# Four graph-network layers on one core: attention weights transposed by DMA bands and VectorE blocks instead of by TensorE

## What is computed

```
L0: e = lrelu((h W1)(h W2)^T), masked by adj; softmax over rows;   relu(attention @ (h W3))
L1: 4 heads, e = lrelu(e_src + e_dst), masked; softmax;            elu(attention @ (h W))
L2: 4 heads, e = Q K^T / 8, masked; softmax;                       layernorm((attention @ V) Wo + bo) * gamma + beta
L3: as L1, with weights and vectors of its own
```

## Time and profile before

| | |
|---|---|
| median of 3 runs | 2933.38 us (2931.53 to 2934.24) |
| the profiled execution, its own time | 2927.78 us |
| its span, first to last instruction | 2926.0 us |
| mean granted TensorE clock | 0.996 |
| DMA packets, bytes | 58840, 109.89 MB |

### The profile page before, as it was taken

One profiled execution on the slowest core, in us unless ns is written; L12 is line 12 of the kernel. 1 busy time (PEld: TensorE's weight loads), 2 busy tenths in 40 slices (PEclk: granted clock), 3 DMA queues, 4 the chain that ended last, 5 costly groups with the idle time before them and its releaser, 6 DMA issues.

```text
span 2926.0 us, 68155 instructions
## 1 busy us (share of the span) xinstructions
PE 2872.5 (98%) x27764; PEld 2045.5 (70%) x27764; DVE 2134.2 (73%) x5596; ACT 1667.6 (57%) x3554; POOL 790.4 (27%) x917
## 2 busy tenths in 40 slices
PE   6899999999999999999999999999999999999988
PEld 5567777767767767767767767767767667767666
DVE  3677877777877777877777877777777777777764
ACT  2456656556656656656656656656656655655633
POOL 2223222323222333222322222323222323222321
PEclk9999999999999999999999999999999999999999
DMA  3011011011011101011101011101011101011000
GB/s 81 24 36 43 24 45 45 33 35 45 24 45 44 37 31 45 23 45 45 38 30 44 23 45 45 38 30 45 23 45 45 37 31 44 23 45 38 30 23 30
DMA packets 58840, 109.89 MB, mean 38 GB/s; under 512 B 5568, under 2 KB 41408, under 8 KB 58528
## 3 DMA queue, kind: packets, MB, share of 16 engines
q1 hardware_dynamic: 58032, 104.61, 10.9%
q0 software_dynamic: 496, 0.92, 0.3%
HBM read 88.21 MB, written 17.30 MB: 36 GB/s over the span
## 4 chain that ended last, share of the span: by engine, by line
PE 94%; DVE 2%; DMA 1%; ACT 1%; issue 1%; POOL 0%; SPq 0%; POOLq 0%; DVEq 0%; ACTq 0%
PE ps L962 20%; PE ps L1069 17%; PE ps L968 11%; PE ps L1095 8%; PE ps L998 8%; PE ps L1128 8%; PE ps L1104 8%; PE ps L1018 8%; PE ps L948 4%; PE ps L1007 2%; PE ps L1115 1%; PE ps L956 1%; DMA hT<-r_dram 1%; DVE pA L746 0%; DVE stats L634 0%
## 5 line engine op out<-in xcount | busy, mean ns | idle before, releaser
L452 ACT COPY hT<-ps 128x1024 f32<-128x1024 f32 x128 | 129.6, 1012 | 431.9 <-PE ps L948 431.9
L746 DVE SCALAR_TENSOR_TENSOR pA<-qT,gval,adjT 128x512 f32<-128x512 f32 x248 | 202.6, 856 | 208.8 <-DMA hT<-r_dram 208.1
L384 POOL TENSOR_TENSOR qx<-qx,xc 128x512 f32<-128x512 f32 x128 | 174.6, 1364 | 647.5 <-ACT qx L524 647.5
L1069 PEld LDWEIGHTS ps<-vals,pA 128*64 128x64 f32 x8192 | 253.9, 139 | 53.1 <-issue 52.8
L1069 PEld LDWEIGHTS ps<-vals,pB 128*64 128x64 f32 x8192 | 249.3, 138 | 59.0 <-issue 59.0
L443 ACT ACTIVATE hn<-xc,nb,rstd 128x256 f32<-128x256 f32 x384 | 202.5, 595 | 140.4 <-DVE nb L651 140.4
L359 POOL TENSOR_SCALAR rstd<-mv 128x4 f32<-128x4 f32 x160 | 37.2, 232 | 880.7 <-DVE mv L643 880.7
L1069 PE MATMUL ps<-vals,pA 128*64 128x65 f32 x8192 | 265.4, 223 | 5.9 <-DVE pA L746 5.9
L1069 PE MATMUL ps<-vals,pB 128*64 128x65 f32 x8192 | 267.0, 224 | 1.0 <-DVE pB L746 1.0
L962 PE MATMUL ps<-wgat,hT 128*128 128x264 f32 x1024 | 255.0, 393 | 0.4 <-ACT hT L452 0.4
L1095 PE MATMUL ps<-qx,qT 64*128 64x512 f32 x1024 | 250.5, 615 | 1.5 <-ACT qx L548 0.9
(11 more groups left out here) (147 smaller groups left out, 6097.3 us busy)
## 6 DMA issues: line engine op xcount, KB each, us to landing
qT<-r_dram SPq DMA_DIRECT2D x64, 512.0 KB, 4.0
hT<-r_dram SPq DMA_DIRECT2D x64, 512.0 KB, 4.9
x_in<-in_x SPq DMA_DIRECT2D x32, 512.0 KB, 3.9
out_x<-xc SPq DMA_DIRECT2D x32, 512.0 KB, 3.0
pX<-in_adj SPq DMA_DIRECT2D x1, 1024.0 KB, 7.2
r_dram<-growT SPq DMA_DIRECT2D x64, 8.0 KB, 1.4
pX<-in_L_gnn_W SPq DMA_DIRECT2D x2, 256.0 KB, 4.7
pA<-in_L_gnn_a POOLq DMA_DIRECT2D x8, 64.0 KB, 7.4
```

Of the source, the lines that this page charges most:

```text
L746: last = nc.vector.scalar_tensor_tensor(out=gat_p[s][h % 2][:, t, :], in0=row, scalar=gval[s][:, 1, t, h:h + 1], in1=adjT[:, t, :], op0=AL ...
L1069: last = nc.tensor.matmul(ps[lo:hi, BANK[f"G{g}.{h}"], t * DV:(t + 1) * DV], gat_p[s][h % 2][:, j, t * P + lo:t * P + hi], vals[s][:, j, h ...
```

## The change

The weights of layer 0 and of heads 2 and 3 of layer 2 are no longer transposed by TensorE. SyncE moves each finished matrix to a scratch tile in 16 DMAs, one for each pair of bands: 32 partitions by one 32-column block out of each 128, which puts every 32 x 32 block where its transpose belongs. VectorE then transposes inside the 32 x 32 blocks, four instructions of 128 x 512 per matrix, back into the tile that held the weights. The scratch of layer 0 and of head 2 is `pB` of the set; head 3 has a new tile `scratch`. Heads 0 and 1 stay with TensorE. `growT` becomes one tile per GAT layer instead of one per set. All banks and the order of all five engines' lists are new; part of layer 3's `gat_norm` and `gat_aggregate` move from c to d, a slot later. In the lists below `...` marks what is left out; the old lists stand above.

```diff
-        probT2 = [[pX[2], pA[s], pB[s], pX[2]] for s in range(SETS)]
+        probT2 = [[pX[2], pA[s], prob2[s][2], prob2[s][3]] for s in range(SETS)]
+        scratch = sb("scratch", [P, NT, N])
-        BY_PE = {(0, 1): (2, 4), (B - 1, 3): (0, 2)}
+        BY_PE = {(0, 1): (5, 7), (B - 1, 3): (1, 2)}
-        pT2_act = [Signal(f"pT2_act{h}", k) for h, k in enumerate((1, 3, 2, 2))]
-        pT2_dve = [Signal(f"pT2_dve{h}", k) for h, k in enumerate((3, 1, 2, 2))]
+        pT2_act = [Signal(f"pT2_act{h}", k) for h, k in enumerate((2, 4, 0, 0))]
+        pT2_dve = [Signal(f"pT2_dve{h}", k) for h, k in enumerate((2, 0, 4, 4))]
+        def scratch2(w, h):
+            return pB[w.s] if h == 2 else scratch
+        def bands(tile, band, column):
+            rows_of = tile[32 * band:32 * (band + 1), :, :].rearrange("p t n -> p (t n)")
+            return rows_of.rearrange("p (j b c) -> p j b c", b=P // 32, c=32)[:, :, column, :]
+        def move(sp, scratch, weights, landed):
+            for a in range(P // 32):
+                for b in range(P // 32):
+                    sp.dma_start(bands(scratch, b, a), bands(weights, a, b)).then_inc(landed.sem, 16)
+            def move0(w):
...
+                p0_ready.wait(sp, w, NT)
+                move(sp, pB[w.s], pA[w.s], moved0)
+            def move2(w, h):
...
+                p2_ready[h].wait(sp, w, NT)
+                move(sp, scratch2(w, h), prob2[w.s][h], moved2[h])
-                spread(b, 1); store(d); spread(c, 3); load_next(a)
+                spread(b, 1); pT2p_ready[1].wait(sp, c, 4); move2(c, 2); store(d); move0(a); load_next(a)
+                spread(c, 3); move2(b, 3)
             def first(a, z):
-                load_next(a)
+                move0(a); load_next(a)
+                gat_values(b, 1); gat_residual(d, 3, 0); gat_residual(d, 3, 1); gat_residual(b, 1, 0)
+                gat_residual(b, 1, 1); deviation(b, 2); plus_beta(b); deviation(c, "in"); residual2(c)
+                deviation(c, 3); residual0(a, 0); residual0(a, 1); deviation(z, 0); deviation(a, 1); gat_values(c, 3)
+            def turned0(w, t):
...
+                moved0.wait(dve, w, 16 * BLOCKS)
+                nc.vector.transpose(pA[w.s][:, t, :], pB[w.s][:, t, :]).then_inc(pT0_dve.sem, 1)
+            def turned2(w, h, t):
...
+                moved2[h].wait(dve, w, 16 * BLOCKS)
+                nc.vector.transpose(prob2[w.s][h][:, t, :], scratch2(w, h)[:, t, :]).then_inc(pT2_dve[h].sem, 1)
```

`weights_transposed0` and both `weights_out0` are removed, and `aggregate0` reads `pA`. The new list of ScalarE:

```diff
+                weights_out2(c, 0, 3); weights_out2(c, 1, 3); gat_exp(b, 1); weights_out2(c, 1, 2)
+                inverse_columns(c, 1); elu_relu(d, 3, 0); elu_min(d, 3, 0); elu_exp(d, 3, 0); elu_relu(d, 3, 1)
+                elu_min(d, 3, 1); elu_m[3].wait(act, d, 2); normalised(a, 0, 0); normalised(a, 0, 1)
+                normalised(a, 0, 2); normalised(a, 0, 3); h_transposed(a, 0); elu_exp(d, 3, 1); inverse_out(c, 0)
+                inverse_out(c, 1); xg_ready[3].wait(act, d, 2); u_out(a); elu_min(b, 1, 0); elu_relu(b, 1, 0)
+                elu_exp(b, 1, 0); elu_relu(b, 1, 1); elu_min(b, 1, 1); elu_exp(b, 1, 1); exp0(a, 0); exp0(a, 1)
+                exp0(a, 2); exp0(a, 3); normalised(b, 2, 0); normalised(b, 2, 1); normalised(b, 2, 2)
+                normalised(b, 2, 3); h_transposed(b, 2); v_out(a, 0); normalised(c, "in", 0); normalised(c, "in", 1)
+                normalised(c, "in", 2); normalised(c, "in", 3); biased_out(b, "KT", 0); biased_out(b, "QT", 0)
+                biased_out(b, "QT", 1); biased_out(b, "KT", 1); normalised(c, 3, 0); normalised(c, 3, 1)
+                normalised(c, 3, 2); normalised(c, 3, 3); relu0(a, 0); relu0(a, 1); relu0(a, 2); h_transposed(c, 3)
+                relu0(a, 3); q_out(c, 3, 0); q_out(c, 3, 1); exp2(b, 1, 0); exp2(b, 0, 0); exp2(b, 0, 1)
+                gat_row_exp(c, 3); normalised(a, 1, 0); normalised(a, 1, 1); normalised(a, 1, 2); normalised(a, 1, 3)
+                gat_exp(c, 3); h_transposed(a, 1); exp2(b, 3, 0); exp2(b, 3, 1); exp2(b, 3, 2); exp2(b, 3, 3)
+                exp2(b, 1, 1); q_out(a, 1, 0); exp2(b, 1, 2); q_out(a, 1, 1); weights_out2(b, 1, 0); exp2(b, 0, 2)
+                exp2(b, 1, 3); exp2(b, 0, 3); v_out(b, 2); exp2(b, 2, 0); exp2(b, 2, 1); inverse_columns(b, 0)
+                weights_out2(b, 0, 2); exp2(b, 2, 2); gat_row_exp(a, 1); weights_out2(b, 1, 1); exp2(b, 2, 3)
```

of VectorE:

```diff
+                gat_weights(d, 3, 3, 0, 1, 2, 3); inverse_sums2(c, 1); gat_norm(d, 3, 0); gat_norm(d, 3, 1)
+                turned2(c, 3, 0); gat_norm(d, 3, 2); gat_norm(d, 3, 3); turned2(c, 3, 1); turned2(c, 3, 2)
+                turned2(c, 3, 3); gat_weights(b, 1, 0, 0, 1, 2, 3); gat_weights(b, 1, 1, 0, 1); gat_out(d, 3, 0)
+                gat_out(d, 3, 1); gat_weights(b, 1, 1, 2, 3); gat_weights(b, 1, 2, 0, 1, 2); norm2(c, 0)
+                gat_weights(b, 1, 2, 3); turned2(c, 2, 0); gat_norm(b, 1, 0); gat_weights(b, 1, 3, 0, 1)
+                masked_max0(a, 0); gat_norm(b, 1, 1); gat_weights(b, 1, 3, 2, 3); masked_max0(a, 1); turned2(c, 2, 1)
+                lrelu0(a, 0); turned2(c, 2, 2); lrelu0(a, 1); gat_norm(b, 1, 2); gat_out(b, 1, 0); masked_max0(a, 2)
+                gat_norm(b, 1, 3); lrelu0(a, 2); turned2(c, 2, 3); masked_max0(a, 3); softmax_shift0(a); second_vectors(a)
+                gat_out(b, 1, 1); lrelu0(a, 3); statistics(b, 2); mean_and_variance(b, 2); norm2(c, 1)
+                shift_of_norm(b, 2); o_out(c); statistics(c, "in"); mean_and_variance(c, "in"); inverse_sum0(a)
+                shift_of_norm(c, "in"); turned0(a, 0); times_gamma(c); turned0(a, 1); turned0(a, 2); statistics(c, 3)
+                mean_and_variance(c, 3); turned0(a, 3); masked_max2(b, 0, 0, 0); masked_max2(b, 0, 0, 1)
+                masked_max2(b, 1, 0, 0); shift_of_norm(c, 3); masked_max2(b, 0, 1, 0); masked_max2(b, 1, 0, 1)
+                masked_max2(b, 0, 1, 1); statistics(z, 0); mean_and_variance(z, 0); masked_max2(b, 0, 2, 0)
+                masked_max2(b, 0, 2, 1); masked_max2(b, 0, 3, 0); masked_max2(b, 0, 3, 1); statistics(a, 1)
+                mean_and_variance(a, 1); shift_of_norm(z, 0); softmax_shift2(b, 0); gat_max_t(c, 3); gat_max(c, 3)
+                masked_max2(b, 1, 1, 0); gat_shift(c, 3); shift_of_norm(a, 1); masked_max2(b, 1, 1, 1)
+                gat_rows_out(c, 3); masked_max2(b, 1, 2, 0); masked_max2(b, 1, 2, 1); masked_max2(b, 1, 3, 0)
+                masked_max2(b, 1, 3, 1); softmax_shift2(b, 1); weights_out2(b, 0, 1); weights_out2(b, 0, 0)
+                gat_weights(c, 3, 0, 0, 1); gat_max_t(a, 1); gat_weights(c, 3, 0, 2, 3); gat_weights(c, 3, 1, 0, 1)
+                gat_max(a, 1); gat_weights(c, 3, 1, 2); inverse_sums2(b, 0); gat_weights(c, 3, 1, 3)
+                gat_weights(c, 3, 2, 0, 1); gat_shift(a, 1); gat_weights(c, 3, 2, 2, 3); gat_rows_out(a, 1)
```

and of TensorE:

```diff
+                pT2_act[0].wait(pe, c); weights_transposed2(c, 0, 3); rT_out[1].wait(pe, b); inverse_spread(c, 0)
+                pT2_act[1].wait(pe, c, 2); gat_aggregate(d, 3, 2); pT2_act[0].wait(pe, c, 2); gat_aggregate(d, 3, 3)
+                gnorm[3].wait(pe, d); inverse_spread(c, 1); aggregate2(c, 0); transposed(a, 0, 0); transposed(a, 0, 1)
+                transposed(a, 0, 2); transposed(a, 0, 3)
                 if a is None and b is not None:
+                    idle_turns(4, 4)
+                gat_aggregate(b, 1, 0); u_columns(a, 0); u_columns(a, 1)
                 if a is None and b is not None:
+                    idle_turns(4, 7)
+                inv_ready.wait(pe, c, 2); gat_aggregate(b, 1, 1); scores0(a, 0); scores0(a, 1); masked0.wait(pe, a)
+                scores0(a, 2)
+                if a is None and b is not None:
+                    idle_turns(3, 4)
+                gat_aggregate(b, 1, 2)
+                if a is None and b is not None:
+                    idle_turns(3, 9)
+                gat_aggregate(b, 1, 3); gnorm[1].wait(pe, b, 3); scores0(a, 3); masked0.wait(pe, a, 3)
+                v_rows(a, 0, 0)
+                if a is None and b is not None:
+                    idle_turns(3, 5)
                 if b is None and c is not None:
+                    idle_turns(4, 29)
+                pT2_dve[2].wait(pe, c, 4); aggregate2(c, 1); v_rows(a, 0, 1)
                 if a is None and b is not None:
+                    idle_turns(3, 4)
+                o_rows(c, 0); o_rows(c, 1); o_rows(c, 2); o_rows(c, 3); transposed(b, 2, 0); transposed(b, 2, 1)
+                transposed(b, 2, 2); transposed(b, 2, 3); v_rows(a, 0, 2); v_rows(a, 0, 3)
                 if a is None and b is not None:
+                    idle_turns(3, 4)
+                o_ready.wait(pe, c); qk_columns(b, "KT", 0); qk_columns(b, "QT", 0); qk_columns(b, "QT", 1)
+                qk_columns(b, "KT", 1); pT0_dve.wait(pe, a); aggregate0(a, 0); pT0_dve.wait(pe, a, 2)
+                aggregate0(a, 1)
                 if a is None and b is not None:
                     idle_turns(4, 5)
```

(23 more changed lines are left out.)

## The result

The changed kernel takes **2969.1 us** (median of 4 runs, 2958.7 to 2970.3) against 2932.5 beside it: a ratio of **1.012**, 95% interval 1.0104 to 1.0136. It is 1.2% slower; forecast were 2832 us and 0.75 for faster. The profiled execution has a span of 2968.2 us.

What follows compares the result with a forecast made beforehand. TensorE, 98% busy, was taken to bound the kernel. From a 2926.0 us span: -158 for removed transposes, +51 for waits, +6 for ends gave 2825, 2827 own time, so 2832 us median; own range 2795 to 2870.

Steps and rivals of the forecast that it cites:

- two prices: Cost of moving a matrix: SyncE's issuing, 384 ns a DMA or 6.1 us, and the DMA engines' packets, 9.0 us.
- The engines' price: DMA engines' time per 128 B packet, 17.6 ns, so 9.0 us a matrix; bounds 3 us and 22 us.
- fixed part f: Size-independent time per DMA packet, 13.6 ns, fitted from two transfers, beside 0.032 ns per byte.
- Point (6): End of slot: move2(b,3) leaves SyncE and the engines free by 81.5, spread(b,1) comes at 83.0; room 1.5 us.
- Point (1): Head 0 of layer 1: VectorE's weights end at 10.2, TensorE wants them at 9.7; wait 0.55 us a slot.
- hand-over: Delay from TensorE to a reader: 0.25 us, 0.16 for the transpose's longer duration and 0.1 for the semaphore.
- Part (D): Rival in TensorE's loop: removed work not all saved because neighbours' weight loads are exposed; called excluded, no chance given.
- Ends: Head and tail outside the loop, and slot 1: about +2 us each, +6 us together.
- point (4): Adjacent gat_max_across(c,3) and gat_max_spread(c,3): TensorE waits 0.85 us, plus 0.3 for transposed(a,1), each slot.
- rival A: Moves outlast their cover at spread(b,1) and turned0: 16 us a matrix, 3117 us; slower than before from 13 us; chance 0.18.

Runs made afterwards that it cites:

- e5: Changed kernel with each matrix moved as 4 straight DMAs of 128 partitions x 2 KB, blocks staying in place; 2847.8 us, 0.9719 of the kernel before.
- e10: Changed kernel with the band DMAs writing to DRAM and VectorE turning each matrix in place; 2945.7 us, 1.0053 of the kernel before.
- e6: Changed kernel with GpSimd instead of SyncE issuing 8 of the 16 band DMAs of move2(b,3); 2870.7 us, 0.9787 of the kernel before.

## Why the prediction was wrong

**The step that failed** is the first of "two prices": SyncE 384 ns a band DMA, from x_in, 6.1 us a matrix. It measured 706 ns and 11.3 us on average, and 12.4 in the slot shown. I had two bounds for the engines and none for SyncE, and its sentence "then SP's 6.1 decides" took the number as known. x_in agrees in packets and in nothing else: it comes from DRAM, spans 128 partitions, and stands alone on its queue. The last of these mattered most, as e5's straight DMAs also take 0.60 to 0.64 in a row. The trace of before even had a hint that I hadn't looked up: of the two broadcasts of the same size, the second, right behind the first, takes longer of SyncE's time. The view of L321 in the kernel before:

```profile
L321 SPq DMA_DIRECT2D qT<-r_dram x64: 319/320/350, 72.5 to 2904.2; - x64
L321 SPq DMA_DIRECT2D hT<-r_dram x64: 422/433/443, 72.9 to 2904.6; - x64
```

**The engines' price** erred to the other side. DMA view of the change, 1379.8 to 1392.3 us:

```profile
q1 hardware_dynamic: 7423, 0.93, 51.2%
```

12.5 us x 16 x 0.512 / 7423 = 13.8 ns a packet of 128 B, against 17.6 taken. The fixed part f of 13.6 ns was too large: in the trace's records of single packets one of 4 B takes 9 ns on average, one of 128 B 13.5 and one of 512 B 35. The price per byte held between the two smallest, and nearly the whole error of 4 ns is in f. The Trainium skill (DMA: Bandwidth & Descriptors, on small descriptors) says that transfers from SBUF to SBUF don't suffer from small descriptors, and the trace agrees; its rule of a read-modify-write under 512 B doesn't show here. Nor does it in e10, whose packets of 128 B go to DRAM and take 13.4 ns. I had weighed the packet's price with care and it was never the bound: the engines are half idle while SyncE is full. In the slot shown a matrix is there 12.4 + 2.3 = 14.7 us after its first DMA instead of 10.4; the mean of the three moves is 13.7.

**Point (6)** had "room 1.5 us" between move2(b,3) and spread(b,1); it became 1.9 us late on average. **Point (1)** therefore: 0.55 us forecast, 3.1 measured. Part of it is a term that the sum lacked: the broadcast was taken at today's 4.9 us though move2(c,2) goes out right behind it, and took 6.2. From growT's copy to the landed row it was 6.8 us before and is 10.7 now: 1.9 of waiting for SyncE, 0.7 by a slower write, 1.3 by the slower broadcast. The 0.1 us "for the semaphore" in the hand-over has no row behind it: in the trace of before VectorE and ScalarE start 0.04 us (median) after the TensorE instruction that they waited for.

**The clock** was not in the forecast at all. Each low stretch costs up to 1.7 or 3.4 us in a slot of 88, 41 us together in the loop, and makes a wait of 3.1 us worth 4.5. I should have asked what a new standstill of TensorE does to a clock that today never falls in the loop.

**The rest of the slot**: 83.4 us instead of 82.3. The removed transposes gave what was forecast, by the time from each TensorE instruction's start to the next: 9.12 us of transposes a slot before, 3.70 after, 5.42 gone (forecast 5.28). But in e5, nearly free of waits, the others are 1.3 us longer than before: scores 0.5, aggregates 0.2, transposes of activations, inverse_spread and gat_max_across 0.5. Part (D), "excluded", was not excluded: not all that was removed is saved. That pieces between which a transpose had stood now meet a hand-over would fit, but no run separates it.

**Ends**: +6 forecast, +16 measured, nearly all before the loop. In e5, where the moves cost SyncE almost nothing, 12 of the 16 remain; they are the new order's. TensorE in the first batches (kernel after):

```profile
82.21 2.08 PE L973 MATMUL ps<-ident,hn 128*128 128x128 f32 x8 [3.80 <-ACT hn L471]
...
114.68 2.16 PE L973 MATMUL ps<-ident,hn 128*128 128x128 f32 x8 [8.34 <-ACT hn L471]
```

These two waits (12.1 us) are for normalised rows while no other batch fills the time; the order before waited for none there and lost 5.7 us at L1069 and 2.3 at L1007 instead. I had gone through the lists for a full slot and estimated the first ones.

**What was right**: the order, by e5 (84.7 us a slot for 84, where shorter waits, 1.2 us for 1.7, and a longer rest partly cancel by luck); the wait before L1058, 0.46 us a slot, part of the 0.85 of point (4); the 32x32 transposes, 0.70 us long and 0.62 apart for the 0.65 taken:

```profile
L852 DVE STREAM_TRANSPOSE pA<-pB 128x512 f32<-128x512 f32 x128 | 85.5, 689 | 112.8 <-DMA pB<-pA 112.8
```

and **rival A's place and sign**. It named spread(b,1) behind move2(b,3), with a break-even at 13 us a matrix (its "23 ns a packet" would be 11.8 us; 13 us is 25 ns), and the kernel came out 1.2% slower. That 13 us is the time for which the run holds up what stands behind it, and SyncE was held 12.0 us by move2(b,3) on average: by its sum the kernel should still have been a little faster, and the slower broadcast, the clock and the longer rest, none of them in it, made it slower. Its cause, slow packets, was the wrong one, and its chance of 0.18 too small for a price whose nearest row differed in source, partitions and neighbours. "Wrong if SP's DMAs take over 0.7 us each" stood in the forecast, and is what happened.

## What to carry to other kernels

Price a DMA on both sides, the engines' packets and the issuing queue's time, and take the latter from DMAs that stand in a row on their queue, not from a single one; a move of many small DMAs is bound by their number, so halve it, or share it between two engines that issue (here that took SyncE's part from 11.3 to 7.6 us, not to half). A queue that carries both a long run of DMAs and a short one that the critical path waits for needs the run's whole length as room. And in a loop where the dense engine never pauses, a new pause of some 2.5 us cost itself and then, in most cases, the half clock behind it, so a forecast has to price both.

## What the runs showed of the hardware

- SyncE's own time for a write of 8 KB or a store of 512 KB is 0.32 to 0.39 us alone and 0.62 right behind a run of others, at the same size; for a band of 32 partitions in a run it is 0.60 to 0.63 in the median and 0.64 to 0.71 on average, whether it has 128, 256 or 512 packets. In e6, where GpSimd issues the other half of a matrix, it is 0.95 on average. The Trainium skill (Perfetto Trace Analysis, DMA Instruction) has the profiled time begin with a wait for the descriptor generator's lock, which would fit a price that depends on what went just before; no run here separates that wait.
- A packet of 128 B takes 13.5 ns of a DMA engine on average from SBUF to SBUF and 13.4 to DRAM (e10); in the change's run of bands the 16 engines were 51% busy.
- A 512 KB broadcast landed after 4.9 us alone, 6.2 with bands behind it and 6.9 with bands on both sides of it, on average.
- TensorE's clock fell to 1.2 GHz for 3.4 or 6.8 us after 22 of 25 standstills of 2.3 us or more, and after none of 1.3 to 1.7 us.
